# One graph block on one core: the small adjacency products are issued in longer runs between the large products of one stage

## The reference

```python
xn = _layernorm(x, axis=-1)
# graph network, twice:   h = x @ W.T + b ; agg = segment_sum(h[src], dst) ; relu(agg)
# mixing (attention):     q = softmax(xn @ Wq.T, -1) * dim**-0.5
#                         k = softmax(xn @ Wk.T, axis=-2) ; v = xn @ Wv.T
#                         context = k.T @ v ; attn = q @ context
#                         y = attn + xn ; mixed = y @ W1.T @ W2.T + y
x = x + gnn(xn, edges) + mixed
x = x + ffn(_layernorm(x))     # 8 experts, Sinkhorn gate, top-k, scatter back
```

## Time and profile before

| | |
|---|---|
| median of 3 runs | 469.3 us |
| the profiled execution | 470.23 us, span 468.5 us, granted clock 0.994 |
| PE busy | 449.9 us (96%) |
| PE weight loads busy | 360.1 us (77%) |
| DVE busy | 321.1 us (69%) |
| ACT busy | 150.9 us (32%) |
| POOL busy | 62.2 us (13%) |

### The profile page before, as it was taken

How to read it: one execution, slowest core, us unless ns; L and a number is a source line. 1 busy time by engine, 2 the same in 40 slices (tenths; PEclk the granted TensorE clock), 3 DMA queues, 4 the chain that set the end, 5 groups by cost and what they waited for, 6 DMA issues and landing times.

```text
span 468.5 us, 6793 instructions
## 1 busy us (share of the span) xinstructions
PE 449.9 (96%) x2414; PEld 360.1 (77%) x2414; DVE 321.1 (69%) x1103; ACT 150.9 (32%) x272; POOL 62.2 (13%) x89
## 2 busy tenths in 40 slices
PE   7999999999999999999999999999999998778995
PEld 3888788888888888888779999877777766544783
DVE  6995699898998988897652110444645656777972
ACT  4686453322323233341222110322132115451120
POOL 4088200000000000000004000002200000005642
PEclk9999999999999999999999999999999989999999
DMA  8902002911000000001200000002744449206791
GB/s 216 279 10 90 1 0 91 218 56 59 1 1 1 1 1 1 1 2 39 88 0 3 1 1 1 1 0 84 266 140 134 133 141 388 100 1 212 265 352 73
DMA packets 20828, 40.45 MB, mean 86 GB/s; under 512 B 2936, under 2 KB 3266, under 8 KB 20787
## 3 DMA queue, kind: packets, MB, share of 16 engines
q1 hardware_dynamic: 18547, 32.55, 22.6%
q0 software_dynamic: 2240, 7.39, 4.3%
HBM read 30.10 MB, written 10.30 MB: 86 GB/s over the span
## 4 chain that ended last, share of the span: by engine, by line
PE 85%; DVE 6%; ACT 3%; issue 3%; DMA 1%; SPq 0%; POOLq 0%; DVEq 0%; ACTq 0%
PE ps L718 46%; PE ps L1014 9%; PE ps L940 9%; PE ps L831 5%; PE ps L705 5%; ACT scrap_a L1405 2%; PE ps L1148 2%; PE ps L1031 1%; DMA X<-in_x 1%; PE ps L863 1%; PE ps L752 1%; PE ps L1118 1%; PE ps L967 1%; PE ps L991 1%; PE ps L1060 1%
## 5 line engine op out<-in xcount | busy, mean ns | idle before, releaser
L1694 DVE TENSOR_SCALAR RING_D<-places,PLACES 125x170 bf16<-125x170 f16 (+1 forms) x239 | 63.1, 264 | 0.0
L1695 DVE TENSOR_SCALAR RING_S<-iota,HOME 125x128 bf16<-125x128 f16 x239 | 59.9, 250 | 0.0
L940 PE MATMUL ps<-AT,H1H 125*128 125x416 f32 (+1 forms) x108 | 38.0, 352 | 0.0
L940 PE MATMUL ps<-AT,H1L 125*128 125x416 f32 (+1 forms) x108 | 38.0, 351 | 0.0
L1014 PE MATMUL ps<-H2H,AT 125*125 125x512 f32 x90 | 36.1, 402 | 0.0
L1014 PE MATMUL ps<-H2L,AT 125*125 125x512 f32 x90 | 35.5, 394 | 0.0
L1031 PE MATMUL ps<-WE0H 128*128 128x512 f32 x119 | 34.0, 421 | 0.0
L1762 DVE TENSOR_TENSOR ps<-ps,bias 125x512 f32<-125x512 f32 x20 | 14.0, 700 | 27.9 <-PE ps L718 27.9
L1841 DVE SCALAR_TENSOR_TENSOR ZL<-ps,ZH 128x416 fp32r<-128x416 f32 (+1 forms) x12 | 6.3, 585 | 38.7 <-ACT ZH L1350 38.7
L705 PEld LDWEIGHTS ps<-RING_D,RING_S 125*125 125x125 bf16 x239 | 25.7, 136 | 7.9
L597 POOL TENSOR_TENSOR G2L<-RAW_G,G2H 128x512 fp32r<-128x512 f32 x4 | 5.0, 1294 | 192.2 <-ACT G2H L1167 192.2
(11 more groups left out here) (408 smaller groups left out, 1177.0 us busy)
## 6 DMA issues: line engine op xcount, KB each, us to landing
RAW_E<-in_experts SPq DMA_DIRECT2D x8, 1024.0 KB, 9.7
RAW_AGAIN<-in_experts SPq DMA_DIRECT2D x3, 1024.0 KB
X<-in_x SPq DMA_DIRECT2D x1, 2240.0 KB
out_x<-X SPq DMA_DIRECT2D x10, 224.0 KB
scratch<-X SPq DMA_DIRECT2D x10, 224.0 KB
scratch<-Y SPq DMA_DIRECT2D x10, 224.0 KB
RAW_K<-in_WkT SPq DMA_DIRECT2D x4, 256.0 KB, 4.6
RAW<-in_mW2T SPq DMA_DIRECT2D x1, 1024.0 KB, 13.3
```

The source lines that it names most:

```text
L940: pe.matmul(place(f), h[0:TT, k, 128 * f:128 * (f + 1)], AT[0:TT, k, c0:c1], start=(k == 0 and n == 0), stop=False)
L1694: V.tensor_scalar(hot_d(v, width(b)), places[0:ET, 0:width(b)], PLACES[0:ET, c:c + 1], None, ALU.is_equal)
L1695: V.tensor_scalar(hot_s(v), iota[0:ET, :], HOME[0:ET, c:c + 1], None, ALU.is_equal).then_inc(done["marked"], 1)
```

## The change

The table that says where the visits stand on PE is built a second time with `runs` true. In it, the two chunks of q{i} (for i from 1 on) are one run at n = 0, the chunks of x{i} at n = 0 and n = 6 are one run of 8 at n = 0, and those at n = 12 and n = 18 are one run of 7 at n = 12. The order of the visits is the same. DVE keeps the old table, so its marks stand where they stood between its other work. q0, the eight products ahead of the stage and h keep their chunks. 

```diff
-def visits_in_products():
+def visits_in_products(runs):
 ...
     for i in range(NT + 1):
         if i < NT:
-            spots += [(f"q{i}", 0, 4), (f"q{i}", 6, 4 if i % 4 == 1 else 3)]
+            q = [(f"q{i}", 0, 4), (f"q{i}", 6, 4 if i % 4 == 1 else 3)]
+            spots += [(f"q{i}", 0, q[0][2] + q[1][2])] if runs and i else q
         if i:
-            spots += [(f"x{i - 1}", n, 3 if n == 12 else 4) for n in (0, 6, 12, 18)]
+            x = [(f"x{i - 1}", n, 3 if n == 12 else 4) for n in (0, 6, 12, 18)]
+            spots += [(f"x{i - 1}", x[n][1], x[n][2] + x[n + 1][2]) for n in (0, 2)] if runs else x
 ...
-CHUNKS_OF_VISITS = visits_in_products()
-VISITS_AT = {(unit, n): vs for unit, n, vs in CHUNKS_OF_VISITS}
+CHUNKS_OF_VISITS = visits_in_products(False)
+VISITS_AT = {(unit, n): vs for unit, n, vs in visits_in_products(True)}
```

Six semaphores of the start of the kernel (`eps_ready`, `zero_ready`, `touched`, `keys_ready`, `sel_ready`, `flag_in`), all raised by DVE, become two that count: `begun` and `tiles_step`. DVE raises them in the order in which the old ones were raised, and each waiter waits for the count that stands for the same instruction:

```diff
-    use("ranks", (5,), ("sel_ready", 1))
+    use("ranks", (5,), ("tiles_step", 3))
-            pe.wait_ge(done["zero_ready"], 1)
+            pe.wait_ge(done["begun"], 2)
-                pe.wait_ge(done["touched"], 1)
+                pe.wait_ge(done["tiles_step"], 1)
-                pe.wait_ge(done["sel_ready"], 1)
-                pe.wait_ge(done["keys_ready"], 1)
+                pe.wait_ge(done["tiles_step"], 3)
-                    pe.wait_ge(done["flag_in"], 1)
+                    pe.wait_ge(done["tiles_step"], 4)
-            act.wait_ge(done["eps_ready"], 1)
+            act.wait_ge(done["begun"], 1)
```

More of the change, by code:

```diff
@@ L415, in gps_block @@
         done = {n: sem(n) for n in (
-            "consts rconsts ranges eps_ready w_hi w_lo_dve w_lo_pool exp_hi el_split dve_chain pool_chain var_ready sqrt_ready inv_ready xf_act xf_dve xnh_ready "
-            "xnl_ready xth_ready xtl_ready grp_ready touched sel_ready home_ready place_key mph_ready mpl_ready "
+            "consts rconsts ranges begun w_hi w_lo_dve w_lo_pool exp_hi el_split dve_chain pool_chain var_ready sqrt_ready inv_ready xf_act xf_dve xnh_ready "
+            "xnl_ready xth_ready xtl_ready tiles_step home_ready place_key mph_ready mpl_ready "
             "k_stored kmax_step diag_ready rmax_ready q_exp q_ready k_shift k_exp eh_ready el_ready "
             "esum_step krs_ready e_used vph_ready vpl_ready th_ready tl_ready cph_ready "
-            "cpl_ready zero_ready keys_ready again_chain marked visited adj_hi q_inv qth_ready qtl_ready mix_added flag_in "
+            "cpl_ready again_chain marked visited adj_hi q_inv qth_ready qtl_ready mix_added "
             "flag_ready again_full again_go zh_ready zl_ready ac_ready ac_used h1_biased h1h_ready h1l_ready h2_biased h2h_ready h2l_ready "
@@ L1499, in peak @@
                     V.tensor_tensor(KMAX[0:TT, :], ps, KMAX[0:TT, :], ALU.max).then_inc(done["kmax_step"], 1)
-            V.memset(eps[:], LN_EPS).then_inc(done["eps_ready"], 1)
+            V.memset(eps[:], LN_EPS).then_inc(done["begun"], 1)
             V.memset(HOT_D[:], 1.0)
-            V.memset(zero[:], 0.0).then_inc(done["zero_ready"], 1)
+            V.memset(zero[:], 0.0).then_inc(done["begun"], 1)
             def edges_of_tiles():
@@ L1567, in row_keys @@
                 link(V.tensor_scalar(keys[0:TP, 1], a, 1.0, None, ALU.add))
-                V.scalar_tensor_tensor(keys[0:TP, 2], a, 1.0, keys[0:TP, 1], ALU.add, ALU.subtract).then_inc(done["keys_ready"], 1)
+                V.scalar_tensor_tensor(keys[0:TP, 2], a, 1.0, keys[0:TP, 1], ALU.add, ALU.subtract).then_inc(done["tiles_step"], 1)
             def touched_blocks():
@@ L1575, in touched_blocks @@
                                                 ALU.is_gt, ALU.mult))
-                dve.sem_inc(done["touched"], 1)
+                dve.sem_inc(done["tiles_step"], 1)
             def choose_tiles():
@@ L1592, in choose_tiles @@
                 link(V.tensor_tensor(left[0:TP], ps, turns[0:TP].unsqueeze(1).broadcast_to([TP, 2, NB]), ALU.is_ge))
-                dve.sem_inc(done["sel_ready"], 1)
+                dve.sem_inc(done["tiles_step"], 1)
             def tiles_left():
                 link(V.tensor_tensor(left[0:TP], left[0:TP], touch[0:TP], ALU.mult))
-                V.tensor_reduce(over[0:TP, 0:1], left[0:TP].rearrange("p h b -> p (h b)"), AX, ALU.add).then_inc(done["flag_in"], 1)
+                V.tensor_reduce(over[0:TP, 0:1], left[0:TP].rearrange("p h b -> p (h b)"), AX, ALU.add).then_inc(done["tiles_step"], 1)
             def chosen_keys():
```

## The result

The changed kernel takes 471.5 us in the median of 7 runs (469.94 to 473.01), the one before 469.77 us beside it. The ratio is 1.0028 with a 95% interval of [1.0015, 1.0042]. A second set of runs gave 1.0031 [1.0008, 1.0054]. The forecast was +0.26%: no change clear of 0.3%, on the slow side of none. Both intervals lie above 1, so the sign is clear. The size agrees with the forecast as far as such an interval can tell: it holds everything from 0.15% to 0.42%. In microseconds the 471.5 lies above the forecast's own range of 470.1 to 470.9, and inside the stated range of 468.6 to 471.8; 0.47 us of the difference are the kernel before, whose median is 469.77 here and was 469.3 when the forecast was made.

The account below looks back on a forecast made before the run. PE bounds the stage, busy 109.00 of 109 us. 1.01 us late after the first tile, 0.26 after 22 more merged runs, 1.22 after x9's wait: 469.3 + 1.2 = 470.5 us; range 468.6 to 471.8, the forecast's own 470.1 to 470.9.

Parts of the forecast that it names:

- the first tile: At q1 and x0, DVE only just ahead: PE waits 0.5, 0.4 and 0.2 us and comes out 1.01 us late.
- middle tiles: Up to q9: no wait, 0.40 us left at n = 12; 22 merged runs bring the lateness to 0.26 us.
- The saving of a merged run: On PE, each of 29 merged runs saves one piece of 0.034 us beside its visits, 0.99 us in all.
- The last tile: At x9's run of seven PE waits 1.1 us for the last mark; the stage ends 1.22 us later.
- the release: PE's start behind a DVE result it waits for: 0.055 us taken, 0.14 kept for the range.
- The sum: Whole kernel: 470.23 + 1.22 = 471.45 us against the profiled execution, 469.3 + 1.2 = 470.5 against the median; chance 0.47.
- Rival 1: In the stage no wait appears and only the saving is left: 468.3 us; chance 0.17.
- Rival 3: On PE, visits past the fourth of a long run are slower: +0.8 us, 471.3 us; chance 0.12.
- the 81 ns of the Trainium skill: Sustained spacing of weight load and matmul pairs on PE at 128 columns; as an estimate +0.6 us, sum 471.1.
- Rival 2: Same waits, but PE starts 0.14 us behind the last mark: 1.40 plus 0.05 for steps, 470.7 to 470.8; chance 0.16.
- Rival 4: Middle tiles lose their 0.40 us of room, eight tiles paying 0.1 each: +0.8 us, 471.3 us; chance 0.04.
- No cost in semaphores, ring, copies, transfers: Costed at nothing: ring waits loosen, ACT's copies stay covered, transfers are needed far later; semaphores bounded at -0.1 and +0.1 us.

Follow-up runs that it names:

- first: Kernel before with only the three runs of q1 and x0 merged; ratio to before 1.0031 [1.0013, 1.0049], stage 107.75 us.
- last: Kernel before with only x9's runs at n = 12 and n = 18 merged; ratio to before 1.0034 [1.0013, 1.0055], stage 107.71 us.
- mid: Changed kernel without its merged runs in q1, x0 and x9's n = 12, 25 merged; ratio to before 0.9995 [0.9981, 1.0009], stage 106.13 us.
- best: Changed kernel, merging only q3 to q9 and x1 to x9, with G1L on DVE behind x9's marks; ratio to before 0.9969, stage 105.96 us.
- halves: Kernel before with old runs in q1 to q9 and x0 to x9 cut in two, 58 runs more; ratio to before 1.0050, stage 108.58 us.
- opener: Changed kernel with the adj_hi wait moved to the first visit of a run; executed once, 471.43 us (before 469.97), stage 108.15 us.
- sems: Changed kernel's semaphores alone (two counting ones for six), all visits at old places; ratio to before 1.0005 [0.9992, 1.0018], stage 106.63 us.

## Why the prediction came out right

The mechanism is the one that was forecast: waits at four known places, and a small saving at each of the others. The size is right in part by luck. The stage became 1.63 us longer, 0.35% of the time, and not 1.22 (0.26%); that the ratio says 0.28% is its scatter.

- *Where the loss comes from.* Shown. The three waits in the first tile (0.53, 0.38 and 0.14 us, forecast 0.5, 0.4 and 0.2) and the one at x9 (1.16, forecast 1.1) appear where they were forecast, middle tiles have none, and first, last and mid separate them (+1.12, +1.08, -0.50).
- *The first tile.* Forecast 1.01 us late, measured 1.08. What was missing: behind a visit that was held, the next large matmul starts 0.08 later (115.23 to 115.31), not 0.03 as in a run that flows. Behind the last run, the only place where no later wait swallows it, it is 0.10 (123.06 to 123.16), and that is the 0.07.
- *The saving of a merged run.* The term that was mis-sized. I took 0.034 us for 22 runs, and the 25 runs between the two places saved 0.61 us, 0.024 each. In the second profile of the changed kernel it is 0.67, 0.027 each, and with mid and best that makes 0.024 to 0.027 in four profiles. The piece itself is right (halves: 0.034). What I left out is that merging doubles the stretch of large matmuls. Over the 24 stretches from 126 to 210 us of the changed kernel the second to fifth step behind a run take 232.2 ns in the mean, and the sixth and all later ones 233.3. Before, with six large matmuls between two runs, there were no such steps. Six of them cost 7 ns a stretch, which brings 0.034 down to 0.027; the rest, down to 0.024 in the first profile, is within what two profiles of one kernel differ by. The shape was in the trace of before: the first graph layer, with one run in 12, has the same 233.3. So PE was 0.55 us late at q9's row maximum, and the last mark of x9 ended 0.54 us late and not 0.26; 0.07 of these 0.28 come from the first tile and 0.21 from the saving.
- *The last tile.* Forecast a wait of 1.1 us, a last visit at 0.055 behind its mark, and +1.22 in all. The wait is there, but the release took 0.14, because this visit also waits for `adj_hi` (shown by opener, in one execution). The order of instructions shown above had it as [waits marked,adj_hi]; I took the 0.14 of the earlier trace rows for chance and left it to a rival. It wasn't chance: in the instruction records of the kernel before, the matmul at 409.56 waits for two semaphores and has a semaphore instruction ahead of it (409.46 to 409.51), and the one at 388.72 waits for one. I priced this rival at 0.09 for each of two places; it came true at the one where it counts, since in the first tile the slow visit (the sixth) has two faster ones behind it that wait for their own marks.
- *The sum.* 1.22 + 0.28 (the last mark later, from both terms above) + 0.09 (release) + 0.02 (the step behind the held visit at x9, 0.050 for 0.03) + 0.02 (the matmuls from there to h0) = 1.63, as measured. The terms missed go in one direction, and only their small size kept the forecast near.
- *Rival 1* (no wait) fell: the waits are in the trace. *Rival 3* fell as it was put: a visit in a long run takes 0.075, (0.69 - 0.24) / 6, the same as in a short one. With it falls the 81 ns of the Trainium skill (TensorE: Matmul & The Clock Gate, section Back-to-back issue gap) as a price for this stream, at least for runs of up to eight. What is slower in the new order is the large matmul: 29 stretches of six steps with 1.1 ns each are 0.2 us, a quarter of the 0.8 that I had priced for this rival. *Rival 2* came half true, with 0.09 at x9 and nothing in the first tile. *Rival 4* didn't occur: in each middle tile the last mark ended 0.46 to 0.48 us ahead of its visit's start.
- *No cost in semaphores, ring, copies, transfers.* Shown inside the stage by sems, and behind it by the 163.06 us. For the semaphores outside the stage it is shown only to within the interval of sems.

## What to carry to other kernels

Work that one engine prepares for another is bunched safely only where the lead is longer than the bunch; an engine's average idle share doesn't say so. Walk the first and the last round of a pipelined loop by themselves, since the lead isn't built up in the one and is eaten by the next stage's work in the other. One misplaced bunch costs (1.1 us here) what some 40 to 45 merged runs bring.

Moving such work later isn't free either: ask what its old place was covering (QTL here).

## What the runs showed that I had not expected

- PE starts a visit 0.055 us behind its mark when it waits for one semaphore, and 0.14 to 0.15 when it waits for two, though the second has long been raised. Moving the second wait to an earlier instruction brings it to 0.055. The second wait is a semaphore instruction of its own in the trace, 0.05 us long.
- Large matmuls in an unbroken stretch step by 233.3 ns from the sixth step on, and by 232.2 in the second to fifth step behind a run of small ones. Why wasn't tried.
- The profiled time of one execution moved by up to 3 us with the arrival of the first inputs (first large matmul at 8.58 to 11.94 us) and with the clock in the Sinkhorn part (first to last sum 14.7 to 16.7 us), far more than the change itself. The distance between two fixed instructions inside the trace told kernels apart: two profiles of the changed kernel have stages of 108.26 and 108.23, before and sems both 106.63.
